# Attention stages two to four: GpSimd's gathers and scatters issued behind P V, and the roots of the two normalisations paired

## What is computed

```python
x = x + tanh(g_xattn[i]) * xattn_i(layernorm(x), ctx, ctx)      # i = 0..3
x = x + tanh(g_ffn[i])   * ffn_i(layernorm(x))
```

## Time and profile before

| | us |
|---|---|
| median of 3 runs (lowest, highest) | 3283.08 (3280.22, 3284.64) |
| the profiled execution | 3315.29, its span 3313.2 |
| busy in it: PE, PEld | 2465.0 (74%), 1858.4 (56%) |
| busy in it: DVE, ACT, POOL | 1675.5 (51%), 1375.5 (42%), 1257.0 (38%) |
| mean granted TensorE clock | 0.797 of full speed |

### The profile page before, as it was taken

The page is one execution under the profiler, slowest core; times in us unless marked ns, Lnnn a source line. Parts: engine busy times, 40 slices in busy tenths (PEclk is TensorE's granted clock), DMA queues, the critical chain, the costliest instruction groups (busy, mean ns, idle before and its releaser), DMA issues. The chain is left out here.

```text
span 3313.2 us, 90488 instructions
## 1 busy us (share of the span) xinstructions
PE 2465.0 (74%) x34265; PEld 1858.4 (56%) x34275; DVE 1675.5 (51%) x4362; ACT 1375.5 (42%) x2620; POOL 1257.0 (38%) x1928
## 2 busy tenths in 40 slices
PE   5999999996866888333369888817992888887680
PEld 4887878775544656222246666614661666765460
DVE  3677767665125666477557555434442344443112
ACT  2555555552224556377635433201222454453220
POOL 1323333334016543377411333350006556653007
PEclk9999999998987878655579877658995677676895
DMA  5000000000431111000010110014551111110343
GB/s 153 17 19 22 23 22 22 20 17 7 136 94 42 38 38 34 11 1 1 4 39 28 36 35 29 24 54 138 164 147 53 34 39 43 42 38 18 110 118 93
DMA packets 211399, 165.91 MB, mean 50 GB/s; under 512 B 30655, under 2 KB 188983, under 8 KB 210976
## 3 DMA queue, kind: packets, MB, share of 16 engines
q1 hardware_dynamic: 194592, 128.45, 13.1%
q0 software_dynamic: 16384, 31.69, 3.4%
HBM read 96.93 MB, written 52.43 MB: 45 GB/s over the span
## 5 line engine op out<-in xcount | busy, mean ns | idle before, releaser
L967 PE MATMUL l_Z<-l_val,l_prob_t 128*64 128x18 f32 x6144 | 336.3, 226 | 46.6 <-issue 45.3
L967 PEld LDWEIGHTS l_Z<-l_val,l_prob_t 128*64 128x64 f32 x6144 | 308.2, 157 | 63.4 <-issue 52.7
L315 POOL DMA_INDIRECT slots<-xn_all,put x256 | 257.2, 1005 | 85.4 <-issue 81.5
L1734 PE MATMUL experts_H<-experts_xs_t,experts_w 128*128 128x512 f32 x576 | 268.9, 611 | 9.2 <-ACT experts_hid L1714 4.9
L200 POOL DMA_INDIRECT l_got<-rows,get x192 | 197.4, 1028 | 184.3 <-PE l_Z L889 117.0
L694 DVE TENSOR_REDUCE l_top<-l_X 128x32 f32<-128x2048 f32 x64 | 146.6, 2290 | 168.5 <-DMA rows<-experts_y 75.3
L1753 PE MATMUL experts_Y<-experts_w,experts_hid 128*128 128x128 f32 x1664 | 197.8, 275 | 4.0 <-DVE experts_hid L1694 2.2
L967 PE MATMUL l_Z<-l_val,l_soft 128*64 128x18 f32 x2048 | 186.0, 244 | 18.6 <-issue 17.7
L721 DVE RECIPROCAL l_recip<-l_Z 128x32 f32<-128x32 f32 x96 | 34.1, 356 | 319.4 <-PE l_Z L967 298.2
L1753 PEld LDWEIGHTS experts_Y<-experts_w,experts_hid 128*128 128x128 f32 x1664 | 191.7, 192 | 6.0 <-issue 6.0
L792 ACT ACTIVATE l_prob_t<-l_Z 128x512 f32<-128x512 f32 x256 | 132.2, 603 | 151.5 <-PE l_Z L895 86.2
(11 more groups left out here) (315 smaller groups left out, 6320.8 us busy)
## 6 DMA issues: line engine op xcount, KB each, us to landing
experts_w<-in_F_w SPq DMA_DIRECT2D x104, 256.0 KB, 2.9
experts_xs<-slots SPq DMA_DIRECT2D x72, 256.0 KB, 2.8
rows<-experts_y SPq DMA_DIRECT2D x72, 256.0 KB, 3.1
l_ctx_t<-in_ctx_t SPq DMA_DIRECT2D x96, 128.0 KB, 2.3
l_q_m<-l_q_t SPq DMA_DIRECT2D x384, 32.0 KB, 1.8
slots<-l_zeros SPq DMA_DIRECT2D x64, 96.0 KB
experts_w<-in_F_w SPq DMA_DIRECT2D x40, 128.0 KB, 2.5
slots<-l_zeros SPq DMA_DIRECT2D x8, 512.0 KB
```

The costliest lines, as they stand in the source:

```text
L315: pool.indirect_dma_start(self.slots, bass.IndirectOffsetOnAxis(ap=g.put[c][:, tile:tile + 1], axis=0), g.xn[:, tile, :], None, bounds_che ...
L967: last = nc.tensor.matmul(Z[64 * tile:64 * tile + 64, 2, 18 * h:18 * h + 18], term[:, t.par(OUT), h // 4, col:col + 64], val[:, t.par(OUT) ...
L1734: nc.tensor.matmul(H[:, c, :], w1_s[:, t.par(2), c, :], xs_t[:, t.par(2), :], start=True, stop=True).then_inc(h_filled[c], 1)
```

## The change

`Router.pool` is cut in three: `scatter`, `add_eps` and `root`. In the first attention (`attention_wide`) they are called in the old order. In the split attentions the step of GpSimd becomes: `var + eps` of the attention's normalisation, `var + eps` of the router's, root of the one, root of the other, `combine`; then a new wait for `o_filled` of this step, that is, for the end of P V; then the scatters, then the gathers. The gather's own wait for `p_filled` is gone. The router's root is called with stage `T0 + 1` in place of `T0`: it belongs to the item whose statistics DVE took one step earlier, and DVE uses it in the step in which it is now computed.

```diff
-    def pool(self, nc, pool, t, s):
+    def scatter(self, nc, pool, t, s):
 ...
+    def add_eps(self, nc, pool, t, s):
         if t.live(s):
             pool.wait_ge(self.w_in, self.loads)
-            wait(pool, self.stats, n0)
+            wait(pool, self.stats, t.done(s))
 ...
+    def root(self, nc, pool, t, s):
+        if t.live(s):
             pool.wait_ge(self.w_in, self.loads)
-            wait(pool, self.eps, n0)
+            wait(pool, self.eps, t.done(s))
 ...
             def step(t):
-                if head and t.live(0):
-
-                    wait(pool, p_filled, t.done(PROB))
-                    head.gather(nc, pool, t, 0, ready, 1)
                 if t.live(NORM):
 ...
                     nc.gpsimd.tensor_tensor(var_eps[...], mv[...], g.eps[:, 0:2], ALU.add).then_inc(eps_done, 1)
+                if tail:
+                    tail.add_eps(nc, pool, t, T0 + 1)
+                if t.live(NORM):
 ...
                     nc.gpsimd.tensor_tensor(rstd[...], var_eps[...], g.neg_half[:, 0:2], ALU.pow).then_inc(rstd_done, 1)
+                if tail:
+                    tail.root(nc, pool, t, T0 + 1)
                 if head and t.live(1):
                     head.combine(nc, pool, t, 1, ready, 1)
+
+                wait(pool, o_filled, t.done(OUT))
                 if tail:
-                    tail.pool(nc, pool, t, T0)
+                    tail.scatter(nc, pool, t, T0)
+                if head and t.live(0):
+                    head.gather(nc, pool, t, 0, ready, 1)
```

More of the change, by code:

```diff
@@ L293, in totals @@
         nc.vector.tensor_tensor(self.g.total_by_row[:, :], self.before[:, :], self.of_batch[:, :], ALU.add)
-    def pool(self, nc, pool, t, s):
-        g, par, k = self.g, t.par(s), self.tiles
+    def scatter(self, nc, pool, t, s):
+        g, k = self.g, self.tiles
         out = s + 5 + self.nb
-        n0 = t.done(s)
         sent_before = t.landed(out + 2, k * self.ks)
@@ L317, in pool @@
                         bounds_check=self.slots.shape[0] - 1, oob_is_err=False).then_inc(self.sent[t.par(out)], 16)
+    def add_eps(self, nc, pool, t, s):
         if t.live(s):
             pool.wait_ge(self.w_in, self.loads)
-            wait(pool, self.stats, n0)
-            nc.gpsimd.tensor_tensor(self.var_eps[:, par, :], self.mv[:, par, :, 1], g.eps[:, 0:k], ALU.add).then_inc(self.eps, 1)
+            wait(pool, self.stats, t.done(s))
+            nc.gpsimd.tensor_tensor(self.var_eps[:, t.par(s), :], self.mv[:, t.par(s), :, 1], self.g.eps[:, 0:self.tiles], ALU.add).then_inc(self.eps, 1)
+    def root(self, nc, pool, t, s):
+        if t.live(s):
             pool.wait_ge(self.w_in, self.loads)
-            wait(pool, self.eps, n0)
-            nc.gpsimd.tensor_tensor(self.rstd[:, par, :], self.var_eps[:, par, :], g.neg_half[:, 0:k],
+            wait(pool, self.eps, t.done(s))
+            nc.gpsimd.tensor_tensor(self.rstd[:, t.par(s), :], self.var_eps[:, t.par(s), :], self.g.neg_half[:, 0:self.tiles],
                                     ALU.pow).then_inc(self.rstd_done, 1)
@@ L1139, in step @@
                                             g.neg_half[:, 0:1], ALU.pow).then_inc(rstd_done, 1)
-                tail.pool(nc, pool, t, 8)
+                tail.scatter(nc, pool, t, 8)
+                tail.add_eps(nc, pool, t, 8)
+                tail.root(nc, pool, t, 8)
             pipeline(pool, ITEMS, 8 + tail.depth(), step, UNROLL)
```

## The result

| | before | after |
|---|---|---|
| median (lowest, highest) | 3283.86 (3280.22, 3293.11) | 3335.7 (3326.31, 3346.59) |
| ratio, 95% interval | | 1.0155, 1.0117 to 1.0192 |
| profiled execution, its span | 3315.29, 3313.2 | 3335.3, 3332.6 |
| mean granted clock | 0.797 | 0.802 |

The change makes the kernel slower by 52 us, where 70 us less were forecast; the range (3110 to 3290) does not hold it.

What follows compares the result with a forecast made beforehand. The prediction took PE completion signals held until GpSimd's indirect issues end, stretched P V and a lowered clock as the bound. 52 + 5 + 23 - 10 = 70 us gave 3213 in the median (3245 profiled); range 3110 to 3290.

Steps and rivals of the forecast that it cites:

- What bounds the kernel (held signals, gaps in P V, low clock): Split attentions: GpSimd's indirect issues delay PE's completion signals (3.8 us a step in l1), stretch P V, and the clock falls.
- The argument that profiling doesn't make them: Whole kernel: profiling would cost about 200 us in l2 and l1, but the profiled execution is only 32 above the median.
- l1, 8.7 us a step: Second attention, two gathers behind P V: step falls from 10.88 to 8.7 us, 52 us gained over 24 steps (35 to 67).
- l2, 16.2 us: Third attention, four scatters behind P V: cost moves to the maxima, step 16.45 to 16.2, 5 us gained (-22 to +93).
- l3, a net gain of 0.9 us a step: Fourth attention: P V gains 2.3 us, held `P` costs up to 2; 25 steps, 23 us gained (-20 to +55).
- The rival "freeze moved", 3343: All three split attentions: late signals move to the maxima and `P` and cost more, sum -60, 3343 us; chance 0.12.
- Its point of decision: That rival is decided by whether the signal of the maxima's transpose falls behind the burst's first issue; l1's step would be 11.2.
- Ramps -10: Filling and emptying steps of l1 and l3, paced by GpSimd's queue: gathers one place later add 0.6 us over 16 steps, 10 lost.
- Paired roots and new wait, zero: GpSimd's step: same root instructions, ready some 5 us ahead of use; only DMAs stand behind the wait for P V; zero cost.
- The port: Behind P V: DVE and GpSimd lock each other out of a shared port, 46 us less gained, 3259 us; rival's chance 0.05.

Runs made afterwards that it cites:

- two pairs of traces: Profiles of the kernel before and of the whole change, taken twice: with the result (spans 3313.2 and 3332.6) and later on one chip (3298.1 and 3348.7).
- plain gathers: Kernel before, with the three split attentions' gathers as plain DMAs of the same bytes, other rows: 3137.84 us, ratio 0.9496 to the kernel before.
- second set: Follow-up runs on one chip that held signals: kernel before 3305.49 us; whole change against it 3350.83 us, ratio 1.0145.
- second pair: Traces of the kernel before and the whole change, one after the other on one signal-holding chip: spans 3298.1 and 3348.7 us.
- control: Later l3 step in the whole change's trace, scatters and router unchanged, gathers run out: the event of `P` comes 0.08 us after its end.
- the four others: First, third, fourth and fifth follow-up sets, on chips that held no signals: kernel before 3085.17, 3093.1, 3090.86 and 3095.05 us.
- the fourth: Follow-up set with kernel before at 3090.86 us; against it, l1 changed and bursts of at most two issues in l2 and l3: 3061.2 us, 0.9918.

## Why the prediction was wrong

* **What bounds the kernel (held signals, gaps in P V, low clock): right for the chip it was read on.** The two pairs of traces and the plain gathers show it. The argument that profiling doesn't make them holds too: in the second set the profiled execution of the change (3350.8) is its median (3350.83). What it left out is that another chip may show none of it: there the old order's l1 step is 8.05 us, not 10.88, and l1's new order costs 0.4 to 0.65% instead of gaining.
* **l1, 8.7 us a step: right** (8.85; 8.90 in the second pair). The stage gained 45.9 us in that pair, where 52 less the ramp were forecast. `P`'s signal, for which the sum allowed 1 us, is not late there (0.01 to 0.02 us in all 24 steps): its last matmul ends behind the two issues.
* **l2, 16.2 us: right that the price moves and stays nearly whole, wrong in where to and in the sign** (16.9; +15 us instead of -5). The maxima (line 744) lost only 24.0 us in 16 waits over 280 us of l2, 1.5 each, not 3.7: the burst stretched the string of `P`, 1.3 to 5.2 us from first to last start. The one case of the earlier trace rows, in which DVE waited 3.71 us for them, was taken as the model and was not the common one. DVE's wait for `S`, behind that `P`, is what grew: 82.1 us over the same window, where 280 us of l2 in the first trace of before have 48.5.
* **l3, a net gain of 0.9 us a step: this is the step that failed.** It was put together of P V free of issues (-2.3) and `P` held up to 2 us, "with a burst of six possibly 4"; the 0.9 lies between 2.3 less 2 and 2.3. Both parts were wrong for the steps with scatters. `P` makes its reader wait 5.2 us longer than in the control in most of them: it ends 4.0 us after the reciprocal and its signal comes 1 us after the sixth issue, at 9.4. The text had the burst's length (7.6 us), its start (0.7 us) and, in the earlier trace rows, a reader that starts 1.05 us after a burst, and so could have had 9.3; instead it took 2 us from the one case of the earlier trace rows, a burst of four that began with `P`, where the signal came while the third issue ran. And P V, free of issues, took 6.9 or 7.0 us in each of those steps and not 3.7, where the first trace of before has 6.5 to 9.2: PE idles while `P` is held (3.97 us ahead of line 953 in the step shown) and has the lower clock in P V, and so little of the 2.3 us is gained. (The 7.5 us of the prediction for P V beside gathers is from first to last start, its 3.7 from first start to last end; by one measure they are 7.5 and 3.5.) On the second pair 13 steps at +4.8 (20.2 from 15.4) are 63 us and 11 at +1.9 (16.7 from 14.8) 21; the last seven give 2 back, which makes the stage's 82.
* **The rival "freeze moved", 3343: nearest to the result (3335.7), and given 0.12.** Its total came near because its errors cancelled: it had l1 at 11.2 us a step and l3 losing only 20. Its point of decision, the maxima's signal in l1, never came into play. l1 and l3 should have been priced apart: in the step of l3 shown `P` starts some 2 us after P V ends and so falls into a burst of 7.6 us, while in l1 it ends behind one of 2.4.
* **Ramps -10: not seen.** The first reciprocal of l1 comes 6.4 us earlier than in the first trace of before, in the second pair at the same time within 0.3 us.
* **Paired roots and new wait, zero: not shown apart.** All outside the three stages sums to -0.2 us, but the roots lie inside them, and no run moves the DMAs without the roots. l2 alone changed, with both in it, changes nothing where no signals are held (1.0005), and l1 has no router and so no second root.
* **The port: right to leave it out of the sum.** In l3 the scatters of the change, all behind P V, take a median of 1043 ns, and 1087 at most; 1005 ns is the mean of all 256 both before and after. The Trainium skill (SBUF — State Buffer, Who interferes with whom) would have them stretched beside DVE; no row here shows it.

The range failed for the same reason as l3: its upper end let l3 lose 20 us, for six issues that hold `P` all through (and left out the 10 us of the ramps). Charged up to the burst's end, by the lengths that the text had, those 13 steps alone could lose 13 x 5.2 = 68 us, by an estimate from the step shown.

## What to carry to other kernels

Where an engine's burst of work holds up signals, moving the burst moves the price to whatever ends inside it: list every completion between the burst's new start and its end, and charge each reader up to the end of the burst, not the delay that one case happened to show. Where signals are held, short bursts at several places beat one long one (two issues at a time were worth 3 us a step in l2, and in l3 while only gathers ran). A part freed of gaps gains little where, behind the stall that was put ahead of it, it runs at the lower clock; and a kernel's losses of this kind should be confirmed on a second chip before they are tuned away.

## What the runs showed of the hardware

* One kernel took 3283 us in the comparison of the result and 3305 in the second set, and 3085 to 3095 us in the four others. The difference is in completions of PE held back, and strings of small matmuls stalled, beside GpSimd's indirect issues: about two in five of the completions in question, against at most one in fifty in the counts made of the others. It is not settled what sets it: a chip listed under the same number (5) was in the second set, which had it, and in the fourth, which had not, and whether those are one chip isn't recorded.
* A held completion mostly comes about 1 us after the last issue of a burst ends (1.05 and 1.02 us above), and so is up to 5.5 us late with six issues. Not always: in 4 of 14 steps with six issues it came while the sixth ran, and in the earlier trace rows while the third of four did.
* It takes indirect issues: beside plain DMAs from the same queue with the same bytes, none of 76 was late on a chip that holds signals, against 44 of 100 beside the indirect ones (one trace).
* In the new order l1's granted clock is 0.98 and l3's 0.60, in one execution, with a mean (0.802) like that of before (0.797): the mean clock says nothing of a change that moves the stalls.
* Not understood: l1 alone changed costs 0.4 us a step there on a chip that holds nothing (194.1 / 23 = 8.44 to 8.05), which is some two fifths of its loss. It is the place and not the indirect form: with plain gathers in the new order the step is 8.39 and 8.44. The rest shows in an unchanged l3, which lasts 418 and 425 us in the two runs of l1 alone and 402 with l2 alone changed.
* Small matmuls stall as well where signals are held: 32 of `P` start over 5.2 us beside scatters and over 1.3 clear of them, 64 of P V over 5.4 and 1.9.
